# A routed mixture of experts: the second layer in fp32, or as three fp32r products of high and low parts

## The chip, the cores and the metric

The kernel runs on one core of one Trainium2 chip. The metric is the time of one execution in microseconds, as the device measures it; the trace of one profiled execution gives a span, from its first to its last instruction, that is a little shorter.

## What is computed

Sixteen sequences of 128 tokens with 256 features pass a cross attention with a residual, and then a feed-forward part with one shared expert and eight routed ones, of which each token takes the best:

```python
out = x + attention(...)
x_n = layernorm(out)
scores_aE = x_n @ router_DE
vals_aK, idx_aK = top_k(scores_aE, 1)
gates = sigmoid(scores where chosen, else -inf).T
routed_in = gates[:, :, None] * x_n[None]
mid = silu(einsum('ead,edf->eaf', routed_in, w1_eDF)) * einsum('ead,edf->eaf', routed_in, w3_eDF)
routed_out = einsum('eaf,efd->ead', mid, w2_eFD)
shared = silu(x_n @ ws1_DF) * (x_n @ ws3_DF) @ ws2_FD
return out + shared + routed_out.sum(axis=0)
```

There are 2048 tokens, E = 8 experts, D = 256, F = 704. The change touches `routed_out` alone, the routed experts' second layer.

## The kernel before

The program has two parts, the attention (to about 454 us of the span) and the experts. The second part computes the shared expert in four groups of 512 tokens (`shared_group`, `shared_out`), chooses an expert for each token, and scatters the tokens, each multiplied by its gate, to a list in DRAM, `xs_sorted`, in which each expert's tokens stand together and each tile of 128 rows belongs to one expert. There are NT = 23 such tiles. Then a routed loop runs over the tiles, two per turn of a hardware loop on each engine, with buffers of even and odd tiles (`par`):

- SyncE reads the tile's expert number from `ETI` and loads its weights: `load_hidden` the first layer's, `W13` (1408 KB), `load_output` the second layer's, `W2` (640 KB for 5 blocks of 128 rows, and 64 KB for the last 64 rows). One queue, in program order: a wait in it holds all loads behind it.
- TensorE: `ex(t)` transposes the tile's tokens, `eh(t)` multiplies them by `W13` (11 blocks of 128 outputs, 2 steps each, fp32), `ey(t)` multiplies the hidden values by `W2` (6 blocks, fp32, 256 columns). The order is `ex(t + 1)`, `eh(t)`, `ey(t - 1)`. The tokens' hidden values lie as stationary operand (128x128), the weights as the moving one.
- ScalarE: `copy_x(t + 1)` takes the transposed tokens out of PSUM and issues the load of the rows of tile t + 3; `routed_act(t)` then takes the silu of the first layer (`SIL`).
- VectorE: `gate_hidden(t)` multiplies by the other half into `MRT`, `output(t - 1)` adds the gathered sum of attention and shared expert.
- POOL (GpSimd) gathers those rows (`gather_base`) and scatters the results to the output.

The shared expert already works with high and low parts: a value is copied to fp32r (the high part) by ScalarE, the difference from it (the low part) is made by VectorE, and `shared_out` multiplies high by high, high by low and low by high in fp32r. The last block has 64 rows only, so its low part lies in the lower half of the partitions of the same tile and two products do. The normalised tokens of the shared expert lie in two fp32r tiles of 128 x 2 x 2048, named `WKV_XTH` and `WKV_XTL` in the rows (they hold the attention's key and value weights first, `XT` in the experts' part); the routed loop doesn't read them.

The semaphores that matter: `t_eh`, `t_ey` (TensorE has finished the first, second layer of so many tiles), `a_es` (silu), `v_em` (gated), `v_ey` (added), `d_w2[par]` (weights landed). The first layer writes PSUM banks of its parity; the second writes bank 7 in all tiles.

Of the kernel before, what the change touches and what calls it, by code (L numbers as in the profile page):

```python
# [24 lines left out]
P = 128  # L25
D = 256
# [14 lines left out]
FT = (F + 127) // 128  # L41
FM = (FT - 1) * 128
FL = F - FM
TOK = NB * P
NT = TOK // P + NE - 1
# [3 lines left out]
NG = TOK // GT  # L49
# [947 lines left out]
def load_w2(sp, dst, tiles, last, done, stacked=False):  # L997

    sp.dma_start(dst[:, 0:FT - 1, :], tiles).then_inc(done, 16)
    sp.dma_start(dst[0:FL, FT - 1, :], last).then_inc(done, 16)  # L1000
    if stacked:
        sp.dma_start(dst[FL:2 * FL, FT - 1, :], last).then_inc(done, 16)


def experts_part(nc, a, mem, out):
    C, IDENT, PS, RTS = mem["C"], mem["IDENT"], mem["PS"], mem["RTS"]
    WS13, WS2, xs, base, XT = mem["WS13"], mem["WS2"], mem["xs"], mem["base"], mem["WKV_XT"]
    ctx = ExitStack()
    with ctx:
        def sb(name, shape, dt=FP32):  # L1010
            return ctx.enter_context(nc.sbuf_tensor(name, shape, dt))

        def sem(name):
            return ctx.enter_context(nc.semaphore(name))
# [4 lines left out]
        W2 = [sb(f"W2_{i}", [128, FT, D]) for i in range(2)]  # L1019
# [26 lines left out]
        WHO = sb("WHO", [128, NT], I32)  # L1046
        XST = [sb(f"XST{i}", [128, KD, P]) for i in range(2)]
        SIL = sb("SIL", [128, FT * P])
        MRT = [sb(f"MRT{i}", [128, FT * P]) for i in range(2)]
        YS = [sb(f"YS{i}", [128, D]) for i in range(2)]  # L1050
        BASE = [sb(f"BASE{i}", [128, D]) for i in range(2)]

# [8 lines left out]
        EY = 7  # L1061
# [16 lines left out]
        t_h = sem("t_h")  # L1078
# [12 lines left out]
        v_pad = sem("v_pad")  # L1091
# [6 lines left out]
        v_em = sem("v_em")  # L1098
        t_ey = sem("t_ey")
# [16 lines left out]
        @block.sync  # L1116
        def _(sp):
            def expert_of(t):
                return sp.value_load(ETI[0:1, t:t + 1] if isinstance(t, int) else ETI[0:1, bass.ds(t, 1)],
                                     min_val=0, max_val=NE - 1)  # L1120

            def load_hidden(t, par, first=False):
                e = expert_of(t)
                if not first:
                    sp.wait_ge(t_eh, t - 1)
                sp.dma_start(W13[par][:, :, :], a["w13"][bass.ds(e, 1), :, :, :].rearrange("a p k f -> p (a k) f"))\
                  .then_inc(d_w13[par], 16)

            def load_output(t, par, first=False):
                e = expert_of(t)  # L1130
                if not first:
                    sp.wait_ge(t_ey, t - 1)
                load_w2(sp, W2[par], a["w2"][bass.ds(e, 1), :, :, :].rearrange("a p k d -> p (a k) d"),
                        a["w2_last"][bass.ds(e, 1), :, :].rearrange("a p d -> (a p) d"), d_w2[par])

            sp.dma_start(X[:, :, :], base.rearrange("(b p) d -> p b d", p=P)).then_inc(d_x, 16)
            sp.wait_ge(v_et, 1)
            for t in range(2):
                load_hidden(t, t, first=True)
# [70 lines left out]
        def _(act):  # L1210
# [27 lines left out]
            def shared_group(g, gate=False, last=False):  # L1238
                for f in range(2):
                    shared_silu(g, f)  # L1240
                if gate:

                    act.wait_ge(v_rt, 4)
                    act.activation(GATE[:, :], BEST[:, :], ACT.Exp, scale=-1.0).then_inc(a_gate, 1)
                for f in range(2):
                    shared_mid(g, f)
                for f in range(2, FT):
                    shared_silu(g, f)
                    if last and f == FT - 2:
                        copy_x(0, 0, free=False)  # L1250
                    shared_mid(g, f)
# [14 lines left out]
            def routed_act(t, par, copy_next):  # L1266

                if copy_next:
                    copy_x(t + 1, 1 - par, free=not (isinstance(t, int) and t == 0),
                           load=not (isinstance(t, int) and t + 3 >= NT))  # L1270
                act.wait_ge(t_eh, t + 1)
                if not (isinstance(t, int) and t == 0):
                    act.wait_ge(v_em, t)
                h = hidden_of(par)
                act.activation(SIL[:, 0:FM], h[:, 0:FM], ACT.Silu)  # L1275
                act.activation(SIL[0:FL, FM:FM + P], h[0:FL, 2 * FM:2 * FM + P], ACT.Silu).then_inc(a_es, 1)  # L1276

            for g in range(1, NG):
                shared_group(g, gate=g == 1, last=g == NG - 1)
            routed_act(0, 0, True)  # L1280
# [6 lines left out]
            routed_act(NT - 1, 0, False)  # L1287

        @block.vector
        def _(dve):  # L1290
# [15 lines left out]
            for par in range(2):  # L1306
                dve.memset(W2[par][FL:2 * FL, FT - 1, :], 0.0).then_inc(v_pad, 1)
                dve.memset(MRT[par][FL:2 * FL, FM:FM + P], 0.0).then_inc(v_pad, 1)
# [137 lines left out]

            def gate_hidden(t, par):
                dve.wait_ge(a_es, t + 1)
                if not (isinstance(t, int) and t < 2):
                    dve.wait_ge(t_ey, t - 1)  # L1450
                h = hidden_of(par)
                dve.tensor_tensor(MRT[par][:, 0:FM], h[:, FM:2 * FM], SIL[:, 0:FM], ALU.mult)  # L1452
                dve.tensor_tensor(MRT[par][0:FL, FM:FM + P], h[FL:2 * FL, 2 * FM:2 * FM + P], SIL[0:FL, FM:FM + P],
                                  ALU.mult).then_inc(v_em, 1)

            def output(t, par, n):

                dve.wait_ge(t_ey, t + 1)
                dve.wait_ge(d_base[par], 16 * (n + 1))
                if not (isinstance(t, int) and t < 2):  # L1460
                    dve.wait_ge(d_y[par], 16 * n)
                dve.tensor_tensor(YS[par][:, :], PS[:, EY, 0:D], BASE[par][:, :], ALU.add).then_inc(v_ey, 1)  # L1462

            gate_hidden(0, 0)
            for t in (1, 2):
                gate_hidden(t, t % 2)
                output(t - 1, (t - 1) % 2, 0)
            with dve.Fori(1, (NT - 1) // 2) as i:
                gate_hidden(2 * i + 1, 1)
                output(2 * i, 0, i)  # L1470
                gate_hidden(2 * i + 2, 0)
                output(2 * i + 1, 1, i)
            output(NT - 1, 0, NT // 2)

        @block.tensor
        def _(pe):
# [94 lines left out]
                last.then_inc(t_eh, 1)  # L1571

            def ey(t, par):
                pe.wait_ge(v_em, t + 1)
                pe.wait_ge(d_w2[par], 32 * (t // 2 + 1) if isinstance(t, int) else 16 * (t - par) + 32)
                if isinstance(t, int) and t == 0:
                    pe.wait_ge(v_pad, 4)
                    pe.wait_ge(v_so, TOK // P)
                else:
                    pe.wait_ge(v_ey, t)  # L1580
                for f in range(FT):
                    last = pe.matmul(PS[:, EY, 0:D], MRT[par][:, P * f:P * (f + 1)], W2[par][:, f, :], start=f == 0,  # L1582
                                     stop=f == FT - 1)
# [68 lines left out]
```

## Time and profile before

| | us |
|---|---|
| three runs | 744.17, 745.23, 754.32 |
| median | 745.23 |
| the profiled execution | 748.07 |
| its span | 746.3 |

| engine | busy us | share of the span |
|---|---|---|
| TensorE, products (PE) | 703.0 | 94% |
| TensorE, weight loads (PEld), beside them | 643.3 | 86% |
| VectorE (DVE) | 428.7 | 57% |
| ScalarE (ACT) | 406.7 | 54% |
| POOL | 177.1 | 24% |

The records of products overlap: one shows when a product runs through the array, and its successor starts before it ends. What a row of products costs is therefore read from the starts, or from the chain of waits, and not from the mean of one.

### The profile page before, as it was taken

To read this page: it belongs to the slowest core of one execution; us is meant where nothing else is said; L and a number is where in the kernel's file an instruction comes from. 1 tells how busy PE (TensorE), PEld (TensorE's weight loads), DVE (VectorE), ACT (ScalarE), POOL (GpSimd) and SP (SyncE) were. 2 spreads that over 40 slices of the span, in tenths; PEclk is the share of its full clock that TensorE was granted. 3 is DMA by queue.
4 is the path that set the end of the run, shared out by engine and by line. 5 is a ranking of instruction groups with operands and counts; after the bars stand their busy time and mean duration, and the time that the engine had idled before them with its cause. 6 is when DMAs were issued, how large, how long until landed. Compare 5 with 4: busy or idle time off the path is not lost. (4 is left out here: it accounts for less than half of the span.)

```text
span 746.3 us, 17165 instructions
## 1 busy us (share of the span) xinstructions
PE 703.0 (94%) x5890; PEld 643.3 (86%) x5890; DVE 428.7 (57%) x904; ACT 406.7 (54%) x1150; POOL 177.1 (24%) x273
## 2 busy tenths in 40 slices
PE   4879999999999999999998978999999999999994
PEld 4778989999898989898897867888898999999994
DVE  5768778887878887788777525375432212121121
ACT  3578687887888787878778654332231112111110
POOL 5431011111111110111344201078202222322222
PEclk9999999999999999999999989999999999999998
DMA  8943443434444343434344323007417998988861
GB/s 305 212 99 91 105 105 102 103 103 103 103 102 105 100 111 95 102 103 105 99 101 122 78 57 121 0 1 265 153 42 262 333 335 304 335 313 339 320 248 37
DMA packets 58306, 114.13 MB, mean 153 GB/s; under 512 B 13020, under 2 KB 33822, under 8 KB 55328
## 3 DMA queue, kind: packets, MB, share of 16 engines
q1 hardware_dynamic: 52272, 104.61, 45.9%
q0 software_dynamic: 2976, 6.31, 2.3%
q10 hardware_dynamic: 3024, 2.76, 1.1%
q8 instruction: 20, 0.33, 0.2%
q14 instruction: 14, 0.11, 0.1%
HBM read 70.62 MB, written 12.34 MB: 111 GB/s over the span
## 5 line engine op out<-in xcount | busy, mean ns | idle before, releaser
L484 ACT ACTIVATE PR<-PS,NMX 128x256 f32<-128x256 f32 x256 | 117.9, 476 | 7.7 <-DVE NMX L643 7.7
L1569 PE MATMUL PS<-XST,W 128*128 128x128 f32 x1012 | 116.8, 276 | 1.4 <-ACT XST L1258 1.4
L1569 PEld LDWEIGHTS PS<-XST,W 128*128 128x128 f32 x1012 | 115.0, 192 | 1.8 <-ACT XST L1258 1.6
L493 ACT ACTIVATE PR<-PR,RINV 128x256 f32<-128x256 f32 x256 | 106.0, 519 | 0.0
L1452 DVE TENSOR_TENSOR MRT<-PS,SIL 128x640 f32<-128x640 f32 x23 | 19.0, 824 | 117.3 <-ACT SIL L1276 117.3
L655 DVE STREAM_TRANSPOSE PR<-PR 128x512 f32<-128x512 f32 x124 | 80.8, 688 | 2.4 <-ACT PR L493 1.7
L879 PE MATMUL PS<-PT,V 128*64 128x128 f32 x1024 | 66.0, 284 | 12.5 <-DMA PT<-PR 12.0
L643 DVE TENSOR_REDUCE NMX<-PS 128x4 f32<-128x1024 f32 x64 | 75.5, 1199 | 1.8 <-PE PS L848 1.8
L791 PE MATMUL PS<-KVH,WKV_XTH 128*128 128x256 f32 x256 | 74.8, 292 | 0.0
L879 PEld LDWEIGHTS PS<-PT,V 128*64 128x64 f32 x1024 | 58.0, 142 | 17.5 <-DMA PT<-PR 8.8
L791 PE MATMUL PS<-KVL,WKV_XTH 128*128 128x256 f32 x256 | 71.9, 281 | 0.0
L791 PE MATMUL PS<-KVH,WKV_XTL 128*128 128x256 f32 x256 | 71.9, 281 | 0.0
L1275 ACT ACTIVATE SIL<-PS 128x640 f32<-128x640 f32 x23 | 16.2, 703 | 101.2 <-PE PS L1569 100.8
L812 PE MATMUL PS<-KVF,WQ 128*128 128x128 f32 x512 | 67.6, 287 | 1.6 <-DVE KVF L624 1.6
L812 PEld LDWEIGHTS PS<-KVF,WQ 128*128 128x128 f32 x512 | 61.5, 197 | 7.2 <-issue 5.1
L357 POOL TENSOR_TENSOR KVL<-KVF,KVH 128x512 fp32r<-128x512 f32 x16 | 20.7, 1293 | 195.5 <-ACT KVH L450 195.5
L1582 PE MATMUL PS<-W,MRT 128*128 128x256 f32 x276 | 63.5, 380 | 0.6 <-DVE YS L1462 0.6
L1582 PEld LDWEIGHTS PS<-W,MRT 128*128 128x128 f32 x276 | 50.8, 191 | 6.8 <-issue 1.0
L484 ACT ACTIVATION_READ_ACCUMULATOR PR<-PS,NMX 128x1 f32 x256 | 54.0, 211 | 0.0
L791 PE MATMUL PS<-WKV_XTH,KVH 128*128 128x512 f32 x128 | 50.8, 397 | 1.9 <-DVE KL L637 1.9
L461 ACT ACTIVATE KH<-PS 128x512 fp32r<-128x512 f32 x64 | 38.3, 598 | 24.8 <-PE PS L791 24.8
L1203 POOL DMA_INDIRECT out_x<-YS,WHO x23 | 23.4, 1019 | 118.4 <-ACT WHO L1260 93.8
(165 smaller groups left out, 1623.5 us busy)
## 6 DMA issues: line engine op xcount, KB each, us to landing
W<-in_w SPq DMA_DIRECT2D x23, 1408.0 KB, 6.0
PT<-PR SPq DMA_DIRECT2D x496, 64.0 KB, 2.0
W<-in_w SPq DMA_DIRECT2D x23, 640.0 KB, 4.8
xs_sorted<-ZERO SPq DMA_DIRECT2D x23, 128.5 KB, 10.2
XS<-xs_sorted ACTq DMA_DIRECT2D x21, 128.5 KB, 4.9
RC<-in_ctx SPq DMA_DIRECT2D x16, 128.0 KB, 2.1
RX<-in_x SPq DMA_DIRECT2D x16, 128.0 KB, 2.1
PR<-in_wkv_t SPq DMA_DIRECT2D x2, 1024.0 KB, 5.9
```

The costliest lines, as they stand in the source:

```text
L357: pool.tensor_tensor(KVL[par][:, :, :], KVF[par][:, :, :], KVH[par][:, :, :].bitcast(FP32), ALU.subtract).then_inc(p_kvl, 1)
L461: act.activation(KH[:, lo:lo + 2, :], twos(PROJ[1 + i]), ACT.Copy).then_inc(a_k, 1)
L484: last = act.activation(probs, logits, ACT.Exp, bias=NMX[:, g, own, p % 2:p % 2 + 1], accum_out=SUM[:, p, own:own + 1])
L493: last = act.activation(probs, probs, ACT.Copy, scale=RINV[:, p, own:own + 1])
L643: dve.tensor_reduce(NMX[:, g, :, :], src, AX.X, ALU.max, negate=True).then_inc(v_mx, 1)
L655: dve.transpose(probs, probs).then_inc(v_tr, 1)
L791: last = pe.matmul(dst, stat(s, k), mov(m, k), start=n == 0, stop=n == len(todo) - 1)
L812: last = pe.matmul(PS[:, PROJ[0], P * j:P * (j + 1)], WQ[:, c, e:e + 128], KVF[par][:, c, P:KEYS], start=c == 0, stop=c == KD - 1)
L879: last = pe.matmul(PS[OWN[own], OB, P * p:P * (p + 1)], V[:, t, e:e + DH], PT[H][:, :, t, 2 * p + own, :], start=t == 0, stop=t == 1)
L1203: pool.indirect_dma_start(out=out, out_offset=bass.IndirectOffsetOnAxis(ap=WHO[:, t:t + 1], axis=0), in_=YS[t % 2][:, :], in_offset=None, ...
L1569: last = pe.matmul(h[:, P * c:P * (c + 1)], lhs13(W13[par], k, c), XST[par][:, k, :], start=k == 0, stop=k == KD - 1)
L1582: last = pe.matmul(PS[:, EY, 0:D], MRT[par][:, P * f:P * (f + 1)], W2[par][:, f, :], start=f == 0, stop=f == FT - 1)
```

## The change

The routed experts' second layer takes the form of the shared one. Per tile, ScalarE copies the hidden values (now `MRF`, one buffer) to fp32r (`MRH`) and VectorE makes the low part (`MRL`; that of the last 64 rows goes to the lower half of `MRH`). The weights are split in the same way, per tile, into `W2H` and `W2L`. These have no memory of their own; they lie in the tokens' tiles `XT`. ScalarE does its part of tile t + 1's weights behind the silu and the hidden values' high part of tile t, VectorE its part behind the low part of tile t. TensorE then does 17 fp32r products in place of 6 fp32 ones.

The buffer `W2[par]` is free once it has been split, so the load waits for `v_w2l` in place of `t_ey`; and it now stands ahead of the first layer's load of the same tile, a tile and a half earlier in the queue than before. The zeroing of the last block's unused half goes away.

```diff
-        MRT = [sb(f"MRT{i}", [128, FT * P]) for i in range(2)]
+        MRF = sb("MRF", [128, FT * P])
+        MRH = [sb(f"MRH{i}", [128, FT * P], FP32R) for i in range(2)]
+        MRL = [sb(f"MRL{i}", [128, FM], FP32R) for i in range(2)]
+
+        W2H, W2L = ([XT[m][:, par, 0:FT * D].rearrange("p (f d) -> p f d", f=FT) for par in range(2)] for m in range(2))
...
                 if not first:
-                    sp.wait_ge(t_ey, t - 1)
+                    sp.wait_ge(v_w2l, t - 1)
...
+            load_output(2, 0)
             load_hidden(2, 0)
             with sp.Fori(1, (NT - 1) // 2) as i:
+                load_output(2 * i + 1, 1)
                 load_hidden(2 * i + 1, 1)
-                load_output(2 * i, 0)
+                load_output(2 * i + 2, 0)
                 load_hidden(2 * i + 2, 0)
-                load_output(2 * i + 1, 1)
-            load_output(NT - 1, 0)
...
+                mid_hi(t, par)
+                if split:
+                    w2_hi(t + 1, 1 - par)
+
+            def mid_hi(t, par):
+                act.wait_ge(v_em, t + 1)
+                if not (isinstance(t, int) and t < 2):
+                    act.wait_ge(t_ey, t - 1)
+                act.activation(MRH[par][:, 0:FM], MRF[:, 0:FM], ACT.Copy)
+                act.activation(MRH[par][0:FL, FM:FM + P], MRF[0:FL, FM:FM + P], ACT.Copy).then_inc(a_mrh, 1)
+
+            def w2_hi(t, par):
+                act.wait_ge(d_w2[par], 32 * (t // 2 + 1) if isinstance(t, int) else 16 * (t - par) + 32)
+                if isinstance(t, int) and t < 2:
+                    act.wait_ge(t_h, FT * NG)
+                else:
+                    act.wait_ge(t_ey, t - 1)
+                act.activation(W2H[par][:, 0:FT - 1, :], W2[par][:, 0:FT - 1, :], ACT.Copy)
+                for half in range(2):
+                    last = act.activation(W2H[par][FL * half:FL * (half + 1), FT - 1, :], W2[par][0:FL, FT - 1, :],
+                                          ACT.Copy)
+                last.then_inc(a_w2h, 1)
...
+            def gate_lo(t, par):
+                dve.wait_ge(a_mrh, t + 1)
+                dve.tensor_tensor(MRL[par][:, :], MRF[:, 0:FM], MRH[par][:, 0:FM].bitcast(FP32), ALU.subtract)
+                dve.tensor_tensor(MRH[par][FL:2 * FL, FM:FM + P], MRF[0:FL, FM:FM + P],
+                                  MRH[par][0:FL, FM:FM + P].bitcast(FP32), ALU.subtract).then_inc(v_mrl, 1)
+
+            def w2_lo(t, par):
+                dve.wait_ge(a_w2h, t + 1)
+                dve.tensor_tensor(W2L[par][:, 0:FT - 1, :], W2[par][:, 0:FT - 1, :],
+                                  W2H[par][:, 0:FT - 1, :].bitcast(FP32), ALU.subtract)
...
+            def routed(t, par, n, split=True):
+                gate_hidden(t, par)
+                output(t - 1, 1 - par, n)
+                gate_lo(t, par)
+                if split:
+                    w2_lo(t + 1, 1 - par)
+
+            w2_lo(0, 0)
             gate_hidden(0, 0)
+            gate_lo(0, 0)
+            w2_lo(1, 1)
...
             def ey(t, par):
-                pe.wait_ge(v_em, t + 1)
-                pe.wait_ge(d_w2[par], 32 * (t // 2 + 1) if isinstance(t, int) else 16 * (t - par) + 32)
+                pe.wait_ge(v_mrl, t + 1)
+                pe.wait_ge(v_w2l, t + 1)
...
+                todo = [(f, s, m) for f in range(FT - 1) for s, m in ((0, 0), (0, 1), (1, 0))]
+                todo += [(FT - 1, 0, 0), (FT - 1, 0, 1)]
```

On SyncE, in the hardware loop's first half, the rows before are these. W13_1 is the first layer's weights of an odd tile t, W2_0 the second layer's of tile t - 1, TENSOR_LOAD reads an expert's number:

```order
L1126 ISA [waits t_eh]
L1126 DMA W13_1<-in_w13 128x2816
L1119 ISA
L1119 TENSOR_LOAD ETI
L1119 ISA x2
L1132 REGISTER_ALU
L999 ISA [waits t_ey]
L999 DMA W2_0<-in_w2 128x1280
L1000 ISA
L1000 DMA W2_0<-in_w2_last 64x256
```

Now, in the same half of the loop (the lines have shifted: 1126 is 1135, 1119 is 1128):

```order
L999 ISA [waits v_w2l]
L999 DMA W2_1<-in_w2 128x1280
L1000 ISA
L1000 DMA W2_1<-in_w2_last 64x256
L1128 TENSOR_LOAD ETI
L1128 ISA x2
L1135 ISA [waits t_eh]
L1135 DMA W13_1<-in_w13 128x2816
```

The load of W2 has moved ahead of the load of W13, for the same tile, and waits for VectorE's split of the tile two before.

On VectorE, in the second half of the hardware loop, these stood for one tile; MRT0 is the gated hidden values of an even tile, YS1 the sum for the tile before:

```order
L1452 TENSOR_TENSOR MRT0<-PS,SIL 128x640 [waits t_ey,a_es]
L1453 TENSOR_TENSOR MRT0<-PS,SIL 64x128
L1462 TENSOR_TENSOR YS1<-PS,BASE1 128x256 [waits d_y1,d_base1,t_ey]
L1468 REGISTER_ALU
L1468 COMPARE_AND_BRANCH
```

And now:

```order
L1481 TENSOR_TENSOR MRF<-PS,SIL 128x640 [waits v_mrl,a_es]
L1482 TENSOR_TENSOR MRF<-PS,SIL 64x128
L1506 TENSOR_TENSOR YS1<-PS,BASE1 128x256 [waits d_y1,d_base1,t_ey]
L1487 TENSOR_TENSOR MRL0<-MRF,MRH0 128x640 [waits a_mrh]
L1488 TENSOR_TENSOR MRH0<-MRF,MRH0 64x128
L1492 REGISTER_ALU
L1493 TENSOR_TENSOR WKV_XTL<-W2_1,WKV_XTH 128x1280 [waits a_w2h]
L1496 TENSOR_TENSOR WKV_XTL<-W2_1,WKV_XTH 64x256 x2
```

The addition stands between the gating and the low part, and the low part of the next tile's weights (W2_1) stands last.

## Rows read from the trace of the kernel before

**Rows 1.** The page: busy us, share of the span and instructions by engine.
```profile
PE 703.0 (94%) x5890; PEld 643.3 (86%) x5890; DVE 428.7 (57%) x904; ACT 406.7 (54%) x1150; POOL 177.1 (24%) x273
```

**Rows 2.** Windows: us, busy us of each engine, granted clock, DMA share, GB/s.
```profile
577.27:716.30 139.03, 139.03 (x1046) 132.67 (x1045) 27.76 (x54) 23.98 (x73) 37.84 (x37) 1.00 0.88 324
641.06:646.56 5.50, 5.50 (x49) 5.40 (x49) 0.42 (x1) 0.47 (x2) 2.04 (x2) 1.00 0.98 392
```

**Rows 3.** The chain that ended last, 560 to 747 us: start, us, what.
```profile
571.94 5.15 PE PS L1569 x44
...
641.70 4.91 PE PS L1569 x44
646.61 2.59 PE PS L1582 x12
...
737.42 0.44 DVE YS L1462
```

**Rows 4.** Timeline of TensorE, the shared second layer: first products of two tiles.
```profile
531.45 0.28 PE L1527 MATMUL PS<-WS2H,MIDH 128*128 128x256 f32 x1
...
533.45 0.28 PE L1527 MATMUL PS<-WS2H,MIDH 128*128 128x256 f32 x1
```

**Rows 5.** Groups by line and form: count, busy us, mean ns of one.
```profile
L1230 ACT ACTIVATE MIDH<-MIDF 128x512 fp32r<-128x512 f32 x20 | 12.3, 630 | 31.8 <-PE PS L1527 20.7 <-DVE MIDF L1391 11.1
L551 ACT ACTIVATE WKV_XTH<-PR 128x1024 fp32r<-128x1024 f32 x4 | 4.0, 1050 | 8.0 <-DMA PR<-in_wkv_t 8.0
L1404 DVE TENSOR_TENSOR MIDL<-MIDF,MIDH 128x512 fp32r<-128x512 f32 x20 | 13.6, 692 | 8.4 <-ACT MIDH L1230 8.3
L332 DVE TENSOR_TENSOR WKV_XTL<-PR,WKV_XTH 128x1024 fp32r<-128x1024 f32 x1 | 1.2, 1215 | 0.0
```

**Rows 6.** Timeline of a tile, all engines, and of the last one, TensorE.
```profile
646.45 2.76 PE L1582 MATMUL PS<-W,MRT 128*128 128x256 f32 x12
646.79 0.34 SPq L1126 DMA_DIRECT2D W<-in_w  x1
...
648.38 0.29 DVE L1453 TENSOR_TENSOR MRT<-PS,SIL 64x128 f32<-64x128 f32 x1
...
731.19 2.76 PE L1582 MATMUL PS<-W,MRT 128*128 128x256 f32 x12
```

**Rows 7.** DMA queues and issues, 577.27 to 716.30 us: KB each, us to landing.
```profile
DMA packets 10914, 45.04 MB, mean 324 GB/s; under 512 B 2028, under 2 KB 5369, under 8 KB 8608
...
W<-in_w SPq DMA_DIRECT2D x18, 1408.0 KB, 5.9
```

**Rows 8.** Timeline of SyncE's queue, weights issued with no wait between them.
```profile
509.42 0.34 SPq L999 DMA_DIRECT2D W<-in_w  x1
...
511.69 0.34 SPq L1126 DMA_DIRECT2D W<-in_w  x1
```

**Rows 9.** Start of the routed part: timeline, and DMA issues of 560 to 565.
```profile
562.62 0.42 DVE L1398 TENSOR_TENSOR X<-PS,X 128x256 f32<-128x256 f32 x1 [1.58 <-PE PS L1527]
...
564.22 0.37 SPq L1126 DMA_DIRECT2D W<-in_w  x1
...
574.68 0.42 DVE L1462 TENSOR_TENSOR YS<-PS,BASE 128x256 f32<-128x256 f32 x1 [4.91 <-DMA BASE<-base,WHO]
...
576.93 2.76 PE L1582 MATMUL PS<-W,MRT 128*128 128x256 f32 x12
...
W<-in_w SPq DMA_DIRECT2D x1, 1408.0 KB, 7.6
```

**Rows 10.** Timeline of POOL, and of VectorE beside it.
```profile
520.04 0.96 POOL L1180 DMA_INDIRECT xs_sorted<-C,POSI  x1 [0.30 <-issue]
521.30 1.26 POOL L1180 DMA_INDIRECT xs_sorted<-C,POSI  x1 [0.30 <-issue]
...
521.03 0.69 DVE L1404 TENSOR_TENSOR MIDL<-MIDF,MIDH 128x512 fp32r<-128x512 f32 x1 [0.70 <-ACT MIDH L1230]
```

**Rows 11.** DMA issues, 511 to 512 us: KB each, us to landing.
```profile
W<-in_w SPq DMA_DIRECT2D x1, 1408.0 KB, 12.1
```

More of the change, by code:

```diff
@@ L1090, in experts_part @@
         p_zero = sem("p_zero")
-        v_pad = sem("v_pad")
+        a_w2h = sem("a_w2h")
+        v_w2l = sem("v_w2l")
+        a_mrh = sem("a_mrh")
+        v_mrl = sem("v_mrl")
         d_base = [sem(f"d_base{i}") for i in range(2)]
@@ L1264, in copy_x, with routed_act @@
                     act.dma_start(XS[par][:, :], tile_rows(xs, t + 2)).then_inc(d_xs[par], 16)
-            def routed_act(t, par, copy_next):
+            def routed_act(t, par, copy_next, split=True):
                 if copy_next:
@@ L1276, in routed_act @@
                 act.activation(SIL[0:FL, FM:FM + P], h[0:FL, 2 * FM:2 * FM + P], ACT.Silu).then_inc(a_es, 1)
+                mid_hi(t, par)
[18 more added lines that the diff above has]
+                last.then_inc(a_w2h, 1)
             for g in range(1, NG):
                 shared_group(g, gate=g == 1, last=g == NG - 1)
+            w2_hi(0, 0)
             routed_act(0, 0, True)
@@ L1286, in _ @@
             routed_act(NT - 2, 1, True)
-            routed_act(NT - 1, 0, False)
+            routed_act(NT - 1, 0, False, split=False)
         @block.vector
@@ L1304, in x_lo @@
                 tokens_lo(dve, XT, PS[:, TRB[t % 2], :], t).then_inc(v_xtl, 1)
-            for par in range(2):
-                dve.memset(W2[par][FL:2 * FL, FT - 1, :], 0.0).then_inc(v_pad, 1)
-                dve.memset(MRT[par][FL:2 * FL, FM:FM + P], 0.0).then_inc(v_pad, 1)
             dve.wait_ge(p_iota, 4)
@@ L1448, in gate_hidden @@
                 dve.wait_ge(a_es, t + 1)
-                if not (isinstance(t, int) and t < 2):
-                    dve.wait_ge(t_ey, t - 1)
+                if not (isinstance(t, int) and t < 1):
+                    dve.wait_ge(v_mrl, t)
                 h = hidden_of(par)
-                dve.tensor_tensor(MRT[par][:, 0:FM], h[:, FM:2 * FM], SIL[:, 0:FM], ALU.mult)
-                dve.tensor_tensor(MRT[par][0:FL, FM:FM + P], h[FL:2 * FL, 2 * FM:2 * FM + P], SIL[0:FL, FM:FM + P],
+                dve.tensor_tensor(MRF[:, 0:FM], h[:, FM:2 * FM], SIL[:, 0:FM], ALU.mult)
+                dve.tensor_tensor(MRF[0:FL, FM:FM + P], h[FL:2 * FL, 2 * FM:2 * FM + P], SIL[0:FL, FM:FM + P],
                                   ALU.mult).then_inc(v_em, 1)
+            def gate_lo(t, par):
[7 more added lines that the diff above has]
+                                  W2H[par][:, 0:FT - 1, :].bitcast(FP32), ALU.subtract)
+                for half in range(2):
+                    last = dve.tensor_tensor(W2L[par][FL * half:FL * (half + 1), FT - 1, :], W2[par][0:FL, FT - 1, :],
+                                             W2H[par][0:FL, FT - 1, :].bitcast(FP32), ALU.subtract)
+                last.then_inc(v_w2l, 1)
             def output(t, par, n):
@@ L1462, in output @@
                 dve.tensor_tensor(YS[par][:, :], PS[:, EY, 0:D], BASE[par][:, :], ALU.add).then_inc(v_ey, 1)
+            def routed(t, par, n, split=True):
[5 more added lines that the diff above has]
+            w2_lo(0, 0)
             gate_hidden(0, 0)
+            gate_lo(0, 0)
+            w2_lo(1, 1)
             for t in (1, 2):
[L1466 to L1472, printed above, removed]
+                routed(t, t % 2, 0)
+            with dve.Fori(1, (NT - 3) // 2) as i:
+                routed(2 * i + 1, 1, i)
+                routed(2 * i + 2, 0, i)
+            routed(NT - 2, 1, (NT - 3) // 2)
+            routed(NT - 1, 0, (NT - 3) // 2, split=False)
             output(NT - 1, 0, NT // 2)
@@ L1573, in ey @@
             def ey(t, par):
-                pe.wait_ge(v_em, t + 1)
-                pe.wait_ge(d_w2[par], 32 * (t // 2 + 1) if isinstance(t, int) else 16 * (t - par) + 32)
+                pe.wait_ge(v_mrl, t + 1)
+                pe.wait_ge(v_w2l, t + 1)
                 if isinstance(t, int) and t == 0:
-                    pe.wait_ge(v_pad, 4)
                     pe.wait_ge(v_so, TOK // P)
@@ L1580, in ey @@
                     pe.wait_ge(v_ey, t)
-                for f in range(FT):
-                    last = pe.matmul(PS[:, EY, 0:D], MRT[par][:, P * f:P * (f + 1)], W2[par][:, f, :], start=f == 0,
-                                     stop=f == FT - 1)
+                mid, w2 = (MRH[par], MRL[par]), (W2H[par], W2L[par])
+                todo = [(f, s, m) for f in range(FT - 1) for s, m in ((0, 0), (0, 1), (1, 0))]
+                todo += [(FT - 1, 0, 0), (FT - 1, 0, 1)]
+                for n, (f, s, m) in enumerate(todo):
+                    last = pe.matmul(PS[:, EY, 0:D], mid[s][:, P * f:P * (f + 1)], w2[m][:, f, :], start=n == 0,
+                                     stop=n == len(todo) - 1)
                 last.then_inc(t_ey, 1)
```

## The prediction

> **What bounds the kernel now.** I read the page first. TensorE is busy 94% of the span, and the next engine 57% [rows 1]. So I asked for the routed stretch by windows, over 18 tiles from one load of the first layer's weights to the 18th after it: 139.03 us, that is 7.724 us per tile, TensorE busy for all 139.03 at a granted clock of 1.00 (2.4 GHz), VectorE 27.8, ScalarE 24.0, and the DMA engines at 0.88 with 324 GB/s [rows 2]. The reader is to see that TensorE has no idle time there at all, and that the DMA engines have little.
>
> The chain of waits says how a tile divides: 44 records of the first layer (22 fp32 products, each of which leaves two records) take 4.91 us and 12 of the second (6 products) 2.59 [rows 3]; the rest of the 7.72, 0.22, is the transposes of the next tile's tokens. The first layer of tile 2 starts at 571.94, behind a wait of about a microsecond. From its end at 576.93 to the end of tile 22's at 731.19 lie 20 periods [rows 3, 6, 9]. Behind that the kernel ends with the second layers of tiles 21 and 22, the last addition at 737.42 [rows 3] and the scatter.
>
> **What the change removes and adds on TensorE.** 6 fp32 products of 256 columns (12 records) become 17 fp32r ones of 256 columns. The same 17 stand in the shared expert's second layer, with the same shapes: tile after tile of 128 tokens begins at 531.45 and 533.45, so 17 products take 2.00 us [rows 4]. That prices the new layer directly: 2.59 - 2.00 = 0.59 us per tile, and 7.72 becomes 7.13. Over the 20 periods that is -11.8 us, if nothing else becomes the bound. The products of tile 0 gain nothing, since what follows them waits for weights (below); those of tiles 21 and 22 are counted with the end.
>
> **The new work on ScalarE and VectorE.** ScalarE copies 512 columns from SBUF in 0.630 us and 1024 in 1.050, so 0.82 ns for a further column; VectorE subtracts 512 in 0.692 and 1024 in 1.215, 1.02 ns each [rows 5]. That gives 0.74 us for 640 columns, 1.26 for 1280, 0.42 for 256 and 0.31 for 128 on ScalarE, and 0.82, 1.48, 0.43 and 0.30 on VectorE. ScalarE's instructions start some 0.10 before the one ahead ends. So the high part of the hidden values costs 0.95, that of the weights 1.90; the low parts cost VectorE 1.13 and 2.38. With what each engine has now (27.8/18 = 1.54 and 24.0/18 = 1.33 us per tile, rows 2) VectorE comes to 5.05 and ScalarE to 4.2 of 7.13 us. Neither is the bound by its sum. What matters is order.
>
> **The path of one tile**, counted from the end of its first layer on TensorE (646.45 in the timeline). The gating (behind the silu) ends at 648.67, +2.22 [rows 6]. The high part of the hidden values ends at +3.2, the low part at +4.35. The second layer of this tile comes only after the next tile's first layer, at +7.13 or later: covered by 2.8 us; only at the kernel's end is there no such cover. The addition of the tile before waits for a second layer that now ends earlier and is done by +2.8, ahead of the low part. Then ScalarE splits the next tile's weights until +5.0, VectorE until +7.43. The token copy, which stands behind that split on ScalarE, ends at about +5.4 of 7.13 and its DMA is issued by +6.2, ahead of the next silu at +7.3.
>
> **The weights' loads.** Before, the queue of SyncE sent the first layer's weights 0.34 us after the first layer's end [rows 6], and the second layer's after the next second layer, 2.59 later; the large load lands after 5.9 (median) [rows 7]. Now the second layer's load of tile t+3 stands first and waits for the subtraction of tile t+1, at +7.43; issued at +7.6. The first layer's load of t+3 stands behind it: between the two issues lay 511.69 - 509.42 = 2.27 us when this pair was issued without a wait [rows 8] (the small load of the last 64 rows and reading the expert's number among them), so with 2.2 I take +9.8. That is 2.7 us after the end of the next first layer, where it was 0.34. It must land before tile t+3's first layer starts, at 2 x 7.13 + 2.00 + 0.22 = +16.5. At 5.9 to 6.0 it lands at +15.8. So this new loop (split, load, first layer of 4.91, three tiles round) gives a period of (9.8 + 6.0 + 4.91)/3 = 6.9 us, just under TensorE's 7.13; a landing time of 6.7 is where they meet. The transfers themselves: 45.04 MB in 18 tiles, 2.50 MB each [rows 7]; where the queue was full it moved 392 GB/s at a share of 0.98 [rows 2], so 6.4 us per tile, or 0.88 x 7.72 = 6.8 by the share. Both are under 7.13, and the load ahead (0.72 MB, 1.8 us at that rate) has a head start of 2.2. I take the period as 7.13 and count nothing for the DMA engines, whose share should rise to about 0.95. That margin, 0.2 to 0.7 us, is the weakest cover here.
>
> **The start.** VectorE's last addition of the shared expert starts at 562.62 and ends at 563.04 [rows 9]; the subtraction of tile 0's weights follows it, to 565.4. The first layer's load of tile 2 was issued at 564.22 [rows 9] and is now issued at 565.4 + 0.2 + 2.2 = 567.8. Before it took until about 571.9, 7.6 us, beside the store of the sums. With 6.0 it lands at 573.8, with 7.6 at 575.4, against the start at 571.94: +1.9 to +3.5. I take +2.0, since the store is out of the way by then. The second layer of tile 0 also waits for both of its parts (to about 568.7), which lies before that landing and costs nothing. The addition for tile 0 waits for gathered rows until 574.68 [rows 9] and holds the low part of tile 1 behind it on VectorE, so tile 2's weights are subtracted at about 578.6 and tile 4's land near 587, just ahead of its start at 588. Cover again, of 1 us.
>
> **The end.** From the last first layer's end to the last addition it was 737.42 - 731.19 = 6.23 us [rows 3, 6]. Now the low part ends at +4.35, the products at about +6.6, the addition starts at +6.8: +0.6.
>
> **Sum.** -11.8 + 2.0 + 0.6 = -9.2 us; bounds -12 (start hidden, 6.8 us of DMA work not felt) and -7.7 (start 3.5). The profiled execution took 748.07 (span 746.3), 2.84 above the median of 745.23. Its own sum is 738.9; against the median it is 736.0, and I forecast that. Two per cent, about what a measurement of this kernel can tell from no change, is 15 us, so this is a gain within it.
>
> **A rule against the change.** POOL spends two descriptor instructions of 37.84/37 = 1.02 us per tile [rows 2] on the gather and scatter, and VectorE now has two-input subtractions from SBUF beside them for 3.5 us of 7.1. Where such a pair met before, POOL's instruction took 1.26 us instead of the 0.96 beside it, and VectorE's took its usual 0.69 [rows 10]: POOL pays 0.3 us, and it is idle most of the time, so I count nothing. If instead VectorE stood still for both instructions, the subtraction would end 2.06 later and the period would be (9.8 + 2.06 + 6.0 + 4.91)/3 = 7.59: 20 x 0.46 = 9.2 us are given back, 745.2. The Trainium skill ("SBUF — State Buffer", section "SBUF: two separate sides") says that VectorE with two SBUF inputs and a GpSimd instruction that reads SBUF take turns on one lock, and that the loser is blocked for the whole instruction. By that, either side could be the one that waits.
>
> **The rivals.**
> - *The loop over the split binds a little.* Landing times of 6.7 to 8.1 us instead of 6.0 give periods of 7.14 to 7.60. For it speaks that the load now has another in front and that the queue is nearly full, with 7.6 us seen at the start [rows 9]; against it that the total is 2.50 MB at 392 GB/s. With a middle value of 7.35: 736.0 + 20 x 0.22 = 740.4, up to 745.4.
> - *VectorE waits for POOL*, as above: 745.2, and less for part of it.
> - *Slower than before*: the landing time itself. When both pairs of loads were in flight together the large one took 12.1 us [rows 11]. In the new order each large load shares the queue with a second one ahead and the tail of the one before. With 12.1 the period is (9.8 + 12.1 + 4.91)/3 = 8.94, and 736.0 + 20 x 1.81 = 772. It decides from a landing time of 8.1 us on (no gain left), and is over 2% slower from 10.3. Against it: those loads were issued 3.6 us apart, beside scatters; these are a whole period apart.
> - *It gains a bit more than forecast*: the start costs nothing and the products run at TensorE's pace: 733.5.
>
> **How the numbers follow.** Forecast 0.57 (733 to 739 as its own range); loop binds a little 0.22; VectorE waits 0.06; slower than before 0.08, of which half by over 2%; more gain 0.07. The lower end takes in the last case with a microsecond of scatter, 732; the upper end takes in most of the second, 744. Above it lie the slow case, the worst of VectorE's wait and of the loop. Faster by over 2% would need 15 us, more than 23 x 0.59 = 13.6 that TensorE could give: 0.02. Slower by over 2%: 0.04. Within: 0.94.
>
> **What would show it.** In the changed kernel's chain the second layer should stand at 2.00 us, 17 records, and the first at 4.91 with nothing between. The interval between loads of the first layer's weights should be 7.13. If it is longer, the wait ahead of tile starts tells which rival: first-layer products that wait for a DMA mean the loop; POOL rows or subtractions longer than 1.26 and 1.48 us mean the lock. The first layer of tile 2 should start near 574, the last addition 6.8 us after the last first layer. The forecast is wrong if the weights' subtraction ends later than about +8.4, or the large load takes over 6.7 us.

## The result and the profile after

| | before | changed |
|---|---|---|
| median of 20 runs, us | 748.37 | 750.94 |
| lowest and highest | 744.17 to 754.32 | 747.95 to 758.20 |
| profiled execution | 748.07 | 749.70 |
| its span | 746.3 | 747.9 |

The ratio is 1.0047, with a 95% interval of 1.0027 to 1.0067: some half a per cent slower (the two medians are 2.6 us apart), where 1.2% faster was forecast. (The median of before over 20 runs is 3 us above that of the three runs shown ahead; against it the forecast would have been 739.2.)

The page of the changed kernel, its first row (busy us, share, instructions, as in [rows 1]):

```profile
PE 693.3 (93%) x6005; PEld 638.5 (85%) x6005; DVE 505.1 (68%) x1015; ACT 471.8 (63%) x1265; POOL 210.2 (28%) x273
```

TensorE has 9.7 us less work than in [rows 1], and the time did not follow. Windows of the changed kernel: the routed stretch, and the start of it (us, busy of PE, PEld, DVE, ACT and POOL, granted clock, DMA share, GB/s, as in [rows 2]):

```profile
590.00:700.00 110.00, 104.61 (x904) 102.67 (x904) 69.96 (x116) 60.86 (x132) 52.62 (x29) 1.00 0.94 328
...
562.00:573.00 11.00, 7.45 (x64) 7.01 (x62) 8.01 (x13) 5.21 (x12) 2.16 (x2) 1.00 0.79 289
573.00:580.40 7.40, 6.70 (x45) 6.73 (x46) 3.68 (x6) 2.24 (x5) 2.31 (x2) 0.77 0.98 329
```

TensorE was busy for every microsecond of the stretch before; now it stands for 5.4 of 110, while the DMA engines are at 0.94 and move hardly more than before (324 GB/s in [rows 2]). From 573 to 580 its granted clock is 0.77, where in the kernel before it was 1.00.

The silu of tile 2 starts at 580.51 and that of tile 22 at 732.51, so a tile takes 7.60 us on average. Most take 7.13 to 7.4, close to the forecast, and eight of the twenty 7.7 to 8.7. The chain that ended last shows what is behind one of these (start, us, what; small pieces left out):

```profile
604.19 1.11 issue
605.30 5.17 PE PS L1622 x44
...
611.09 0.27 ACT SIL L1285
...
612.22 0.30 DVE MRF L1482
...
613.19 0.29 ACT MRH L1295
613.48 1.16 ACT WKV_XTH L1303
...
617.24 0.43 DVE WKV_XTL L1496
617.83 0.34 SPq L999
...
619.61 8.62 DMA W<-in_w
628.27 5.18 PE PS L1622 x44
```

This is the loop that the prediction drew: first layer, silu, gating, split of the next tile's weights on ScalarE and VectorE, then the release of the second layer's load, the first layer's load behind it, and the first layer three tiles on. From 610.5 (the end of the first layer's records) the large load is issued 9.1 us later and lands after 8.62; with the first layer's 5.18 that is 22.9 us for three tiles, or 7.65 each. The whole stretch shows the same in its medians (the changed kernel's DMA issues, 590 to 700 us: KB each, us to landing, as in [rows 7]):

```profile
W<-in_w SPq DMA_DIRECT2D x14, 1408.0 KB, 8.6
W<-in_w SPq DMA_DIRECT2D x14, 640.0 KB, 4.2
```

### The profile page after: what moved, and what is told of

The parts are those of the page before. It is cut to its first block and busy times, and to the rows that moved or that the text cites. A ratio compares the mean times of both kernels' runs of the same rounds, so it can differ in the third digit from the quotient of the medians.

```text
span 747.9 us, 17640 instructions
## 1 busy us (share of the span) xinstructions
PE 693.3 (93%) x6005; PEld 638.5 (85%) x6005; DVE 505.1 (68%) x1015; ACT 471.8 (63%) x1265; POOL 210.2 (28%) x273
## 3 DMA queue, kind: packets, MB, share of 16 engines
q10 hardware_dynamic: 3024, 2.76, 1.2%
## 5 line engine op out<-in xcount | busy, mean ns | idle before, releaser
L1622 PE MATMUL PS<-XST,W 128*128 128x128 f32 x1012 | 119.4, 278 | 10.1 <-issue 8.6
L1622 PEld LDWEIGHTS PS<-XST,W 128*128 128x128 f32 x1012 | 116.5, 194 | 12.6 <-issue 10.3
L879 PE MATMUL PS<-PT,V 128*64 128x128 f32 x1024 | 64.8, 281 | 10.9 <-DMA PT<-PR 10.4
L1203 POOL DMA_INDIRECT BASE<-base,WHO x23 | 48.5, 2110 | 45.0 <-DMA base<-X 38.3
L1212 POOL DMA_INDIRECT out_x<-YS,WHO x23 | 31.7, 1377 | 88.2 <-DVE YS L1506 88.2
L350 POOL TENSOR_TENSOR VE<-MV,EPST 128x1 f32<-128x1 f32 (+1 forms) x48 | 9.3, 193 | 151.1 <-DVE MV L591 73.9
L791 PE MATMUL PS<-WKV_XTL,KVH 128*128 128x512 f32 x128 | 50.7, 396 | 0.0
L791 PE MATMUL PS<-WKV_XTH,KVL 128*128 128x512 f32 x128 | 50.7, 396 | 0.0
```

The costliest lines, as they stand in the source:

```text
L791: last = pe.matmul(dst, stat(s, k), mov(m, k), start=n == 0, stop=n == len(todo) - 1)
L879: last = pe.matmul(PS[OWN[own], OB, P * p:P * (p + 1)], V[:, t, e:e + DH], PT[H][:, :, t, 2 * p + own, :], start=t == 0, stop=t == 1)
L1203: pool.indirect_dma_start(out=BASE[t % 2][:, :], out_offset=None, in_=base, in_offset=bass.IndirectOffsetOnAxis(ap=WHO[:, t:t + 1], axis=0 ...
L1212: pool.indirect_dma_start(out=out, out_offset=bass.IndirectOffsetOnAxis(ap=WHO[:, t:t + 1], axis=0), in_=YS[t % 2][:, :], in_offset=None, ...
L1622: last = pe.matmul(h[:, P * c:P * (c + 1)], lhs13(W13[par], k, c), XST[par][:, k, :], start=k == 0, stop=k == KD - 1)
```

## The experiments

After the result I held three theories of the lost gain.
- **A, throughput.** The DMA engines can't deliver a tile's 2.50 MB in less than about 7.5 us, whatever the order.
- **B, order.** They can, but the first layer's load now comes late and behind the other, so it lands late for TensorE.
- **C, POOL.** VectorE's subtractions hold up POOL's descriptor instructions, and these hold up the transfers.

In what follows a period is the start of the silu of tile 22 less that of tile 2, over 20. Those of the three in question: before 7.71, changed 7.60, and 7.13 was forecast. (The last tile has no transposes of a next one ahead of it, which takes 0.01 off the mean.) Where a load is given as "+9.4", that is counted from the end of the first layer three tiles ahead of its own, as in the prediction. Each ratio is to runs of the kernel before that were made together with those of the kernel in question (medians 748.47 and 747.29 us).

### Less TensorE work in the old order

```diff
-                for f in range(FT):
+                for f in range(5):
                     last = pe.matmul(PS[:, EY, 0:D], MRT[par][:, P * f:P * (f + 1)], W2[par][:, f, :], start=f == 0,
-                                     stop=f == FT - 1)
+                                     stop=f == 4)
```

The other kernel has 4 and 3 in the two places.

> The kernel before, with the routed second layer over 5 of its 6 blocks (the last 64 rows of the hidden values are left out of the sum; all loads stay). TensorE alone then needs 7.72 - 0.43 = 7.29 us per tile. Theory A (the DMA engines cannot deliver a tile's 2.50 MB in less than about 7.5 us, in whatever order): period 7.5, 20 x 0.22 = 4 us less than before in all. Theory B (the changed kernel lost its gain by the order and the late release of its loads, which this kernel doesn't have): period 7.29, some 9 us less than before.

> The same with 4 of 6 blocks in the routed second layer (the last 192 rows left out of the sum; all loads stay): TensorE alone 6.86 us per tile, below anything the changed kernel could ask. Theory A: period 7.5 as with 5 blocks, DMA share near 1. Theory B: period 6.9 to 7.0, some 15 to 18 us less than before; the DMA engines' own floor by the page of before, 6.8, would just be touched.

Measured: periods of 7.28 and 6.88, ratios to before 0.9855 [0.9804, 0.9906] and 0.9752 [0.9703, 0.9801], from two runs each. But for the last tile, with 5 blocks every tile takes 7.29 to 7.30; with 4 one takes 7.50 and the others 6.86. The window 590 to 700 us of the kernel with 4 blocks:

```profile
590.00:700.00 110.00, 109.59 (x863) 105.29 (x862) 24.67 (x48) 21.34 (x64) 32.75 (x32) 1.00 0.97 362
```

The DMA engines deliver the same bytes per tile at 362 GB/s, one tile every 6.9 us. Theory A falls. At the same time 0.97 says that little is left below 6.9; a period of 7.13 is inside what they can do.

### The products without the split

```diff
-                    sp.wait_ge(v_w2l, t - 1)
+                    sp.wait_ge(t_ey, t - 1)
...
-                if split:
+                if split and isinstance(t, int) and t == 0:
                     w2_hi(t + 1, 1 - par)
...
-                if split:
-                    w2_lo(t + 1, 1 - par)
```

(and SyncE's loads in the order of before)

> The changed kernel with the weights' split done for tiles 0 and 1 only (later tiles are multiplied by those weights, so the routed output is another one), and the loads in the order and with the waits of before; 17 fp32r products and the hidden values' split stay. TensorE 7.13 us per tile. Theory A: period 7.5. Theory B: period 7.13, 20 x 0.59 less than before, about 11 us. Theory C (VectorE's two-input subtractions lengthen POOL's descriptor instructions to 2.26 and 1.40 us and slow the transfers): 7.13 to 7.2 too, with POOL's instructions back near 1.1.

Measured: period 7.15, every tile but the last 7.13 to 7.18; 743.50 us, ratio 0.9937 [0.9900, 0.9975]. The 17 products cost what the prediction said. The total gains less than the loop: the second layer of tile 0 waits for the split of tile 1's weights as well here, TensorE stands for 3.90 us ahead of it, and the granted clock from 573 to 580 us is 0.77. Its large load, 590 to 700 us:

```profile
W<-in_w SPq DMA_DIRECT2D x15, 1408.0 KB, 7.5
```

The order and the waits are those of before, and still the load lands after 7.5 and not after the 5.9 of [rows 7]. The kernel with 5 blocks shows the same (7.6 at a period of 7.28). So a part of the longer landing comes with the shorter period alone, in the old order. It costs nothing here, since the load leaves at +7.5: (7.5 + 7.5 + 4.91)/3 = 6.6.

### The first layer's load ahead again

```diff
-            load_output(2, 0)
             load_hidden(2, 0)
+            load_output(2, 0)
             with sp.Fori(1, (NT - 1) // 2) as i:
-                load_output(2 * i + 1, 1)
                 load_hidden(2 * i + 1, 1)
-                load_output(2 * i + 2, 0)
+                load_output(2 * i + 1, 1)
                 load_hidden(2 * i + 2, 0)
+                load_output(2 * i + 2, 0)
```

> The changed kernel, whole, with one edit: the first layer's load of a tile is issued ahead of the second layer's again (the second layer's still waits for the split). Theory A: period still 7.5, and only the start is better by about 3 us (load of tile 2 issued near 564 again, no idle of 3.4 us, no fall of the clock). Theory B: period 7.13 and the start as before: some 10 us less than before. Theory C: period as in the changed kernel, since the subtractions and POOL still meet.

Measured: period 7.11 (7.16 in nearly every tile; the mean is a little lower because ScalarE, behind its splits, takes up the silu of tile 2 late; by the ends of the first layers it is 7.15), 736.88 us, ratio 0.9837 [0.9800, 0.9874]. All the split's work is in it. This is the gain of the forecast and a little more, 11.6 us instead of 9.2, from the changed kernel by exchanging lines; the period is the one forecast, and the start costs nearly nothing (the first layer of tile 2 begins 9.39 us after that of tile 1, in the kernel before 9.30). Windows of this kernel, and its loads from 590 to 700 us:

```profile
573.00:580.00 7.00, 7.00 (x64) 7.00 (x64) 4.96 (x9) 3.63 (x9) 3.27 (x2) 1.00 1.00 384
590.00:700.00 110.00, 110.00 (x970) 110.00 (x969) 75.30 (x124) 63.59 (x137) 51.46 (x31) 1.00 0.96 349
...
W<-in_w SPq DMA_DIRECT2D x16, 1408.0 KB, 7.0
W<-in_w SPq DMA_DIRECT2D x16, 640.0 KB, 6.7
```

TensorE has no idle time left in these stretches, and the clock holds at the start. The large load leaves at +7.5 instead of +9.4 and lands after 7.0 instead of 8.6. POOL's instructions are as long as in the changed kernel in nearly every tile (below), so theory C can't be what costs the period.

### Order alone, without the split's work

```diff
-                    sp.wait_ge(v_w2l, t - 1)
+                    sp.wait_ge(t_eh, t - 1)
+                    if isinstance(t, int):
+                        sp.wait_ge(v_w2l, 2)
```

(on top of the kernel that splits once, with the loads in the order of the changed kernel)

> Loads in the order of the changed kernel (second layer's ahead of the first layer's), but with no split per tile (split for tiles 0 and 1 only, so the routed output is another one) and the second layer's load waiting for the first layer two tiles back, so that the pair is issued 7.5 and 9.3 us after the end of a tile's first layer, about as in the changed kernel (7.6 and 9.4). If order and place in the queue cause the loss: landing 8 to 8.6 us, period (9.3 + 8.3 + 4.91)/3 = 7.5. If it is the split's work on VectorE and ScalarE, or what it does to POOL: period 7.16 as in the kernel that splits once. The start is later here, so only the period counts.

Measured: period 7.76, tiles of 7.1 to 8.8 as in the changed kernel; 761.26 us, ratio 1.0177 [1.0110, 1.0245], from two runs, much of it from the start. SyncE's queue in this kernel and then in the changed one, one pair of loads each:

```profile
649.12 0.33 SPq L999 DMA_DIRECT2D W<-in_w  x1
649.63 0.49 SPq L1000 DMA_DIRECT2D W<-in_w_last  x1
650.90 0.34 SPq L1135 DMA_DIRECT2D W<-in_w  x1
```

```profile
649.18 0.34 SPq L999 DMA_DIRECT2D W<-in_w  x1
649.70 0.49 SPq L1000 DMA_DIRECT2D W<-in_w_last  x1
650.96 0.34 SPq L1135 DMA_DIRECT2D W<-in_w  x1
```

The two loads stand 1.78 us apart in both, and the large one lands after a median of 8.1 us. (That the times themselves are alike is chance.) The loss is there although VectorE is busy 38 of 110 us instead of 70 and POOL's gather takes 1.03 us again. So neither the split's work nor what it does to POOL is needed to make the period long. The place was not quite the one intended: the release hangs on TensorE's own first layer here, so every delay comes back, and the large load leaves at +9.2 to +10.9, at a median of +10.0 instead of +9.3. But already +9.2 with a landing time of 8.1 asks for (9.2 + 8.1 + 4.91)/3 = 7.4. The order of the loads, with the later issue that it brings, is enough.

### Late, but in front

```diff
             def load_hidden(t, par, first=False):
                 e = expert_of(t)
                 if not first:
                     sp.wait_ge(t_eh, t - 1)
+                if not first:
+                    sp.wait_ge(v_w2l, t - 1)
```

(on top of the kernel with the first layer's load ahead)

> The kernel with the first layer's load ahead, whole, but that load now also waits for the split (v_w2l), as the pair did in the changed kernel: issued at +7.6 instead of about +7.5. If what hurts is to stand behind the other load (1.8 us later, and 0.72 MB in front): landing about 7.0, loop (7.6 + 7.0 + 4.91)/3 = 6.5, period 7.16, and only the start loses 1 to 2 us. If what hurts is the release by VectorE: period near 7.6 again.

Measured: period 7.22 (by the ends of the first layers 7.26), 741.02 us, ratio 0.9919 [0.9882, 0.9955]. 0.38 of the 0.49 us between 7.60 and 7.11 come back. Single tiles take 6.3 to 9.2, and the landing time is 7.6. But the load was not issued at +7.6 as expected. The second layer's load now stands behind the large one, its last 64 KB land late, and ScalarE waits for them ahead of the weights' split, in eight of the fifteen tiles from 590 to 700 us, 8.6 us in all. One of them:

```profile
645.02 1.27 ACT L1305 ACTIVATE WKV_XTH<-W 128x1280 fp32r<-128x1280 f32 x1 [1.08 <-DMA W<-in_w_last]
```

So the split ends later than in the changed kernel, and the large load leaves at a median of +8.6 (from +7.6 to +11.1). That is 1.1 us later than in the kernel with the load ahead and 0.8 earlier than in the changed one, and it lands 1.0 us sooner than there. A release by VectorE with the large load in front thus keeps most of the gain; what remains lost comes at least in part from waits of the split for the small load (the one long wait of TensorE, 1.79 us at 700.3, is for a load issued behind a split that had waited 1.51 us for it). The start lost 0.7 us: the first layer of tile 2 begins behind a wait of 1.66 us instead of 0.98.

### The same place in the queue, fewer bytes ahead

```diff
-                load_w2(sp, W2[par], a["w2"][bass.ds(e, 1), :, :, :].rearrange("a p k d -> p (a k) d"),
-                        a["w2_last"][bass.ds(e, 1), :, :].rearrange("a p d -> (a p) d"), d_w2[par])
+                n = FT - 1 if first else 1
+                sp.dma_start(W2[par][:, 0:n, :], a["w2"][bass.ds(e, 1), :, 0:n, :].rearrange("a p k d -> p (a k) d"))\
+                  .then_inc(d_w2[par], 16)
...
```

> The changed kernel with the second layer's load cut from 640 KB to 128 KB from tile 2 on (one block of five; the others keep the weights of tiles 0 and 1, so the routed output is another one). Issue times stay at +7.6 and +9.4. If the bytes in front make the landing long: landing 6.0 to 6.5, period 7.16. If late issue alone were enough: period stays above 7.3.

Measured: period 7.15, every tile but the last 7.13 to 7.17; 740.78 us, ratio 0.9898 [0.9873, 0.9924]. Its DMA issues, and its window:

```profile
W<-in_w SPq DMA_DIRECT2D x16, 1408.0 KB, 6.3
W<-in_w SPq DMA_DIRECT2D x16, 128.0 KB, 2.4
```

```profile
590.00:700.00 110.00, 110.00 (x970) 110.00 (x970) 74.93 (x124) 63.67 (x140) 54.88 (x30) 1.00 0.80 274
```

The large load is issued as late as in the changed kernel (+9.4, 1.8 us behind the other) and lands after 6.3 instead of 8.6, and (9.4 + 6.3 + 4.91)/3 = 6.9 is covered. This kernel also moves a fifth less in all (274 GB/s), so by itself it doesn't say whether the bytes hurt by being ahead or by being there; the kernel with the first layer's load ahead shows that they can be there at no cost when that load leaves at +7.5. Not shown is what late issue alone would cost with all the bytes. In the kernels that send them all, the large load first, it lands after 7.0 to 7.9 us, and from +9.4 that would ask for 7.1 to 7.4. The late issue and the longer landing both come with the new order, and no run here takes them apart. The start keeps an idle time like the changed kernel's, 3.23 us.

### A candidate: the last tile in fp32

```diff
-            ey(NT - 1, 0)
+            pe.wait_ge(v_em, NT)
+            pe.wait_ge(d_w2[0], 16 * (NT + 1))
+            pe.wait_ge(v_ey, NT - 1)
+            for f in range(FT):
+                w = fwidth(f)
+                last = pe.matmul(PS[:, EY, 0:D], MRF[0:w, P * f:P * (f + 1)], W2[0][0:w, f, :], start=f == 0,
+                                 stop=f == FT - 1)
```

(on top of the kernel with the first layer's load ahead; the splits of the last tile go)

> The kernel with the first layer's load ahead, whole, with the last tile's second layer in fp32 as before the change (no split on its path). The low and high parts of the last hidden values go (about 2.1 us), the product is 0.6 longer: 1.6 us less than the kernel with the first layer's load ahead, 735.3 where that was 736.9. Both theories say the same; it is a candidate that would beat both kernels.

Measured: 735.28 us, ratio 0.9827 [0.9779, 0.9875]. From the last silu to the last addition it takes 725.57 - 719.89 = 5.68 us, where the kernel with the load ahead takes 726.15 - 719.65 = 6.50. That is 0.8 less and not the 1.6 expected. The row of its last products, on TensorE:

```profile
722.51 3.02 PE L1669 MATMUL PS<-W,MRF 128*128 128x256 f32 x12 [0.64 <-DVE YS L1507]
```

The expectation overlooked that the fp32 products then wait for the addition of the tile before, which frees their bank of PSUM, 0.64 us; the twelve records take 3.02 us behind that wait instead of 2.76. The two kernels can't be told apart by their ratios; both beat the kernel before, by 1.6 and 1.7%. In this one the large load lands after 7.9 us and not 7.0, with the same order and the same waits: landing times of one order scatter by that much.

## Why the prediction was wrong, point by point

**The products: right.** One tile's second layer takes 2.00 to 2.03 us in the chain of the changed kernel, against 2.00 forecast from the shared expert.

**The work on the other engines: right.** VectorE's 1280 columns took 1.492 us (1.48 by the slope), ScalarE's 1.254 (1.26), 640 columns 0.825 and 0.737. The chain in the routed stretch ran as drawn: in the stretch of a tile whose first layer ended at 641.56, the second layer's load for three tiles on left at 649.18, +7.62 where +7.6 was forecast.

**The loads: the step that failed.** "At 5.9 to 6.0 it lands at +15.8" took the landing time of before for a kernel with a shorter period and another order. In the changed kernel the median is 8.6. The old order at a period of 7.15 already gave 7.5 (the products without the split), over the 6.7 where the prediction's two limits meet; the new order gave the rest. The form of the loop was right, and so was its threshold: with the measured issue at +9.4 and 8.6 it gives (9.4 + 8.6 + 4.91)/3 = 7.64 us, and 7.60 was measured. The prediction named this case as its rival, with landing times of 6.7 to 8.1, and priced 8.1 as no gain; it put 0.22 on it and took the other one on the word of two figures. The first was 392 GB/s, read from a stretch of 5.5 us in which the queue was full [rows 2]; over 110 us no kernel here moved more than 362, and the changed kernel moved 328 at a share of 0.94. (At 362 a tile's 2.50 MB still take only 6.9 us, so the rate was not the bound.) The second was that the load ahead had "a head start of 2.2" us for bytes worth 1.8: the head start was 1.78, and it did not come out of the landing time. Why the large load lands 2.3 us later with 704 KB ahead of it than with 192 KB (8.6 and 6.3), where the 0.52 MB between them would take 1.3 us at 392 GB/s, is not settled, nor why the same bytes take longer in one order: with the large load ahead, the last 64 KB were in about 1.6 + 7.4 = 9.0 us after the first issue, in the other order the large load was in after 1.8 + 8.6 = 10.4. It isn't the rate alone: the kernel with 4 blocks moved more per us than any other and landed its large load, which stands first, after 7.0. The trace gives no row per DMA engine that would tell more.

**The start: size wrong, and one term missing.** It was priced at +2.0. From the timeline of the changed kernel, the load of tile 2, its landing time, and the first layer of tile 2:

```profile
566.45 0.38 SPq L1135 DMA_DIRECT2D W<-in_w  x1
W<-in_w SPq DMA_DIRECT2D x1, 1408.0 KB, 7.2
...
573.70 6.78 PE L1622 MATMUL PS<-XST,W 128*128 128x128 f32 x44 [3.42 <-issue]
...
580.23 0.36 PE L1637 MATMUL PS<-WKV_XTH,MRH 128*128 128x256 f32 x1
```

The first layer of tile 2 began at 573.70, 1.76 us later than in [rows 3], where 573.8 was forecast. That the number came out so close is luck: the load left at 566.45 and not at 567.8, and took 7.2 us and not 6.0. This trace also stood 0.76 us earlier at the first layer of tile 1, so the real delay is 2.5. And TensorE had stood for 3.42 us ahead of it, its granted clock fell to 0.77 over the next stretch, and the first layer took from 573.70 to 580.23, 6.53 us instead of 4.99. This second price, 1.5 us, was nowhere in the sum. In the kernel with the first layer's load ahead the idle time is 0.98 us and the clock stays at 1.00.

**The end: right.** The last addition starts at 739.02, the first layer of tile 22 ended at 732.23: 6.79 us, against the 6.8 forecast.

**The sum, put right.** Against the profiled execution of before: the part ahead of the routed loop 0.76 earlier (by the starts of the first layer of tile 1, 561.88 and 562.64); the end of tile 2's first layer 580.23 - 576.93 + 0.76 = +4.06; 20 periods of 7.60 instead of 7.71, 152.00 - 154.26 = -2.26; the end +0.56. Together +1.6, and the executions differ by 749.70 - 748.07 = 1.63. Of the forecast's -9.2, 9.5 us are missing in the periods and 2.1 in the start. Two figures of the prediction don't add up by its own terms: with the start at no cost, -11.8 + 0.6 is -11.2 and not the -12 of its bounds, and against the median that gives 734.0 and not 733.5. Neither changes the outcome.

**The rule against the change: half right.** POOL's rows in the changed kernel, and in the one with the order alone, where VectorE subtracts only the hidden values:

```profile
645.14 1.43 POOL L1212 DMA_INDIRECT out_x<-YS,WHO  x1 [4.25 <-DVE YS L1506]
...
646.88 2.27 POOL L1203 DMA_INDIRECT BASE<-base,WHO  x1 [0.30 <-issue]
```

```profile
644.08 1.40 POOL L1214 DMA_INDIRECT out_x<-YS,WHO  x1 [5.31 <-ACT WHO L1271]
645.78 1.03 POOL L1205 DMA_INDIRECT BASE<-base,WHO  x1 [0.30 <-issue]
```

POOL's instructions grow from 1.02 us to 1.4 and 2.27: by 0.4 beside 0.8 us of VectorE's subtractions, by 1.25 beside 2.2 us of them. VectorE's do not grow (1.49 for 1280 columns). The prediction said that POOL pays and that it costs nothing. It pays four times as much as forecast (1.25 and not 0.3 for the gather), and in these kernels that costs nothing indeed: gathers of the same length stand in the kernel with a period of 7.11. The Trainium skill ("SBUF — State Buffer", section "SBUF: two separate sides") has the loser of the lock blocked for the whole instruction. The trace agrees in that POOL loses where VectorE began first, but it loses about half of the time beside it and not all. Where the gather began first, neither side grew, as here in the kernel with the load ahead:

```profile
603.31 1.02 POOL L1203 DMA_INDIRECT BASE<-base,WHO  x1 [0.30 <-issue]
603.90 1.49 DVE L1493 TENSOR_TENSOR WKV_XTL<-W,WKV_XTH 128x1280 fp32r<-128x1280 f32 x1 [1.50 <-ACT WKV_XTH L1305]
```

No row here shows VectorE as the loser; the longest of these subtractions took 1.55 us.

**Slower than before** was given 0.08 with a landing time from 8.1 on. That case came, at 8.6, but not quite as drawn: at the measured issue of +9.4 the periods gain nothing only from 8.5 on, and by themselves they still gained 2.3 us. What made the whole slower is the start (+4.1) and the end (+0.6), which the prediction had at +2.6 together.

## What to carry to other kernels

When a queue of loads is nearly full, the order of two loads in it is worth as much as their bytes: put the one that the bounding engine waits for in front, and read a landing time only from a row with the same load ahead of it and at the period that is forecast. A landing time from a slower loop is too short for a faster one. A rate from a few full microseconds is no capacity; take the bytes of many periods, or cut the compute and see how fast the loads then follow. And a wait of 3.2 us and more ahead of TensorE cost more than itself here, since the work behind it started at the lower clock; waits up to 1.8 us did not.

## What was not expected of the hardware

- The same load of 1408 KB landed after very different times, and both the period and the order count. Medians: 5.9 us in the kernel before (period 7.71); in its order 7.6 and 7.5 at periods of 7.28 and 7.15, and 7.0 at 6.88, where less is computed; 7.0 and 7.9 in two kernels with 704 KB issued 1.1 us behind it; 8.6 and 8.1 with 704 KB issued 1.8 us ahead; 6.3 with 192 KB ahead and a fifth fewer bytes in all.
- The record group of a first layer lasted its usual 5.15 us behind an idle time of 0.98 to 1.66 us, 6.78 behind 3.23 and 3.42 us, and 7.82 behind 4.30 us (which followed one of 3.90, with 4.0 us of products between). At 0.77 the granted clock is a mean over a stretch of both levels, 1.2 and 2.4 GHz. The later idle times in the changed kernel, 0.3 to 1.3 us ahead of eight tiles, left the granted clock at 1.00.
- The runs of the changed kernel spread over 10.3 us, with granted clocks of 0.975 to 0.989, in the main the slower the lower.
